# Attention heads on one core: the exponentials turned by fp32 products with the identity instead of transposes

## The chip, the cores and the metric

The kernel runs on one core of a Trainium2 chip. The time is the device time of one execution in microseconds (us). The profile calls the engines PE (TensorE, matrix products; PEld are its weight loads), DVE (VectorE), ACT (ScalarE), POOL (GpSimd) and SP (SyncE). TensorE runs at 2.4 GHz or 1.2 GHz, whichever the chip grants; the profile shows this as a granted clock of 1.00 or 0.50.

## What is computed

Three stages follow each other: an oscillator network with a feed-forward layer, an attention layer with 16 heads of 16 columns over 512 tokens for each of 8 batches, and a mixture of experts. Only the attention is touched:

```
att = einsum('bhqd,bhkd->bhqk', Q, K) / sqrt(Dh) + b[0]
att = att * m + (1.0 - m) * NEG_INF
att = softmax(att, axis=-1)
y = einsum('bhqk,bhkd->bhqd', att, V)
```

TensorE sums over the partition axis. The exponentials come out with the queries q on the partitions, and the product with V needs the keys k there, so each head's 512 x 512 matrix of exponentials has to be turned: 16 tiles of 128 x 128.

## The kernel before

Each engine has its own queue, written out by hand in the function `attention`, and the queues meet only at semaphores. There are 8 x 16 = 128 heads; `all_heads` runs `step(b, h)` over them on each engine. A head is cut into four query tiles (`qt`) and four key tiles (`kc`) of 128.

For head h the work goes round like this:

- PE `scores` (L1021): one product 64 x 128 by 64 x 512 per `qt` into one of two PSUM banks `Lps`. It waits until DVE has emptied that bank two scores ago (`s_neg`).
- DVE `negate_and_max` (L1111): adds the mask term, writes the negated scores `negL` and their minimum `nM` (`s_neg`).
- ACT `exps` (L1081): the exponentials `Pr` in fp32 (`s_exp`).
- PE `transposes` (L1031): for one `kc` it turns the four tiles of `Pr` of the head before into one PSUM bank `Tps[kc]`. The first `kc` of a head waits for all four exponentials of that head (`s_exp`), and each waits for the bank's last reader on DVE (`s_lo`).
- ACT `transposed_high` (L1088) copies `Tps[kc]` to fp16, and DVE `transposed_low` (L1131) writes what the fp16 copy lost.
- PE `values` (L1043, L1046): 32 small products with V, for the head two back; then DVE `invert_sums` (L1119) and `normalize` (L1125), and POOL `split_output` (L979).

The order on PE in one step is score 0, score 1, kc 0 and 1, score 2, kc 2 and 3, score 3, values. The order on ACT is copy of kc 0, copy of kc 1, exponential 0, copy of kc 2, exponential 1, copy of kc 3, exponentials 2 and 3. The order on DVE is minimum 0, minimum 1, low part of kc 0, minimum 2, low part of kc 1, minimum 3, low parts of kc 2 and 3, normalize. Copies and low parts belong to the head before the one whose scores run. When a batch ends, POOL adds up the next batch's mask term `negC` (L947) after the last minimum of the batch, and DVE waits for it before its first minimum of the new batch.

In the first stage the function `transform` (L273) has the program's only other fp32 products: 16 of them, 128 x 128 by 128 x 512, into the tiles the profile calls `up`.

Of the kernel before, what the change touches and what calls it, by code (L numbers as in the profile page):

```python
# [22 lines left out]
P = 128  # L23
# [657 lines left out]
def attention(nc, x1_dram, qk_dram, mask, b0, w_qk, ident, moe_up, WU, YH, YL):  # L681
# [3 lines left out]
    with ExitStack() as ctx:  # L685
        def sb(name, shape, dt=F32):
            return ctx.enter_context(nc.sbuf_tensor(name, shape, dt))
# [9 lines left out]
        with ExitStack() as c1:  # L697
# [30 lines left out]
            @block.sync  # L728
            def _(sp):
                sp.dma_start(wst[:], w_qk).then_inc(in_w, 16)  # L730
                with sp.Fori(0, B // 2) as bb:
                    for j in range(2):
                        b = bb * 2 + j
                        sp.wait_ge(x_lo, b + 1)
                        sp.dma_start(xb[:, j], x1_dram[b]).then_inc(in_x[j], 16)
# [108 lines left out]
        idS = sb("idS", [P, P])  # L844
# [9 lines left out]
        Pr = sb("Pr", [P, 2, DC, D])  # L854
# [5 lines left out]
        Tps = [ctx.enter_context(nc.psum_tensor(f"Tps{i}", [P, 512], F32)) for i in range(4)]  # L860
# [42 lines left out]
        def before(b, h, d):  # L903

            return (b, h - d) if h >= d else (b - 1, h - d + NH)

        def all_heads(eng, step):

            for h in range(NH):
                step(0, h)  # L910
            with eng.Fori(1, B) as b:
                for h in range(NH):
                    step(b, h)
            for h in range(3):
                step(B, h)

        def exists(b, h, d):

            if not isinstance(b, int):
                return True  # L920
            return 0 <= b * NH + h - d < B * NH
# [89 lines left out]
        @block.tensor  # L1011
        def _(pe):
            for s in (s_T, s_pv):
                pe.sem_inc(s, AHEAD)
            pe.wait_ge(in_id, 32)

            def scores(b, h, qt):
                n = (b * NH + h) * DC + qt
                base = 64 * (h % 2)
                pe.wait_ge(s_neg, n - 1 + AHEAD)  # L1020
                pe.matmul(Lps[qt % 2][:, :], QR[base:base + 64, h // 2, qt * P:(qt + 1) * P],  # L1021
                          KR[base:base + 64, h // 2, :], start=True, stop=True).then_inc(s_L, 1)

            def transposes(b, h, kc):
                i = b * NH + h
                if kc == 0:
                    pe.wait_ge(s_exp, i * DC + DC + AHEAD)

                pe.wait_ge(s_lo, DC * i + kc - DC + 1 + AHEAD)
                for qt in range(DC):  # L1030
                    last = pe.transpose(Tps[kc][:, qt * P:(qt + 1) * P], Pr[:, h % 2, qt, kc * P:(kc + 1) * P], idS[:])  # L1031
                last.then_inc(s_T, 1)

            def values(b, h):
                i = b * NH + h
                pe.wait_ge(s_lo, DC * i + DC + AHEAD)
                pe.wait_ge(s_norm, i - 1 + AHEAD)
                for qt in range(DC):


                    out = Ops[h % 2][:, qt]
                    for kc in range(DC):
                        pe.matmul(out[:, 0:VW], PT[:, h % 2, 0, kc, qt * P:(qt + 1) * P], V[:, b, kc, h],  # L1043
                                  start=(kc == 0), stop=False, skip_group_check=True)
                    for kc in range(DC):
                        last = pe.matmul(out[:, DH:VW], PT[:, h % 2, 1, kc, qt * P:(qt + 1) * P], V[:, b, kc, h, DH:VW],  # L1046
                                         start=False, stop=(kc == DC - 1), skip_group_check=True)
                last.then_inc(s_pv, 1)

            def step(b, h):  # L1050
                def score(qt):
                    if exists(b, h, 0):
                        if h % (NH // 2) == 0 and qt == 0:
                            pe.wait_ge(qk_in[h // (NH // 2)], b * QKI + QKI)
                        scores(b, h, qt)

                def transpose(kc):
                    if exists(b, h, 1):
                        transposes(*before(b, h, 1), kc)

                for qt, kcs in ((0, ()), (1, (0, 1)), (2, (2, 3)), (3, ())):
                    score(qt)
                    for kc in kcs:
                        transpose(kc)
                if exists(b, h, 2):
                    values(*before(b, h, 2))

            all_heads(pe, step)
# [372 lines left out]
```

## Time and profile before

| what | value |
|---|---|
| time, median of 3 runs | 3174.29 us (3158.02 to 3213.94) |
| the profiled execution, device time | 3180.47 us |
| its span, first to last instruction | 3178.8 us |
| busy: PE, DVE, POOL, ACT | 85%, 80%, 42%, 39% of the span |
| first and last transpose (L1031) start at | 1801.4 and 2620.0 us |
| granted clock, mean of the span | 0.882 |

Times of single instructions are those of the one profiled execution. A matrix product's duration in the profile runs from its start until its last result is out, so durations of neighbouring products overlap; the spacing of their starts tells how many fit into a stretch. A row "x8" of the timeline merges eight instructions into one piece, from the first start to the last end.

### The profile page before, as it was taken

How to read it: one execution, taken by the hardware profiler on the slowest of the kernel's cores; microseconds unless marked ns; L12 is line 12 of the kernel's file. 1: busy time of each engine (PE TensorE's matmuls, PEld its weight loads, DVE VectorE, ACT ScalarE, POOL GpSimd, SP SyncE). 2: the span in 40 equal slices, each digit the busy share in tenths (PEclk: the TensorE clock that was granted, in tenths of full speed). 3: DMA queues.
4: the chain of work that ended last, by engine and by line, in shares of the span. 5: the costliest groups of instructions: out<-in, count | busy, mean ns of one | idle time of the engine just before them, and what ended most of it. 6: DMA issues, size and time to landing. Idle time of an engine off the chain costs nothing. (4 is left out here: it accounts for less than half of the span.)

```text
span 3178.8 us, 116365 instructions
## 1 busy us (share of the span) xinstructions
PE 2693.4 (85%) x41104; PEld 1859.3 (58%) x41104; DVE 2549.3 (80%) x11914; ACT 1240.1 (39%) x4102; POOL 1350.6 (42%) x3951
## 2 busy tenths in 40 slices
PE   4478888888888888888887788899998995999999
PEld 4356666666666666666665455566665662444444
DVE  7989999999999999999994698877788776544545
ACT  3343333333333333333333587766677660000000
POOL 6845566666565665555552233322333226000000
PEclk6599999999999999999998898855568557999999
DMA  4100000000000000000003411011111101000000
GB/s 177 51 6 10 3 10 10 10 10 7 7 10 10 10 10 4 10 10 10 10 3 127 126 45 43 17 45 32 29 31 45 32 1 67 0 27 26 0 26 13
DMA packets 43922, 88.98 MB, mean 28 GB/s; under 512 B 7168, under 2 KB 23808, under 8 KB 41600
## 3 DMA queue, kind: packets, MB, share of 16 engines
q1 hardware_dynamic: 36336, 63.11, 6.2%
q10 hardware_dynamic: 4752, 10.49, 0.9%
q0 software_dynamic: 2304, 8.39, 0.8%
q8 instruction: 324, 5.31, 0.7%
q14 instruction: 206, 1.69, 0.2%
HBM read 65.18 MB, written 16.78 MB: 26 GB/s over the span
## 5 line engine op out<-in xcount | busy, mean ns | idle before, releaser
L228 PE MATMUL rest<-Tl,CW 128*128 128x56 f16 x16384 | 618.5, 190 | 317.2 <-DVE Tl L494 317.0
L228 PEld LDWEIGHTS rest<-Tl,CW 128*128 128x128 f16 x16384 | 503.1, 97 | 564.2 <-DVE Tl L494 560.2
L347 ACT ACTIVATE Tf<-X 128x32 f32<-128x32 f32 x768 | 176.0, 229 | 781.4 <-DVE X L538 781.4
L1031 PE MATMUL Tps<-idS,Pr 128*128 128x128 f32 x2048 | 421.5, 373 | 52.0 <-ACT Pr L1081 41.9
L1111 DVE CUSTOM_DVE_ANT_0 negL<-Lps,negC 128x512 f32<-128x512 f32 x512 | 341.4, 685 | 140.5 <-PE Lps L1021 133.4
L1031 PEld LDWEIGHTS Tps<-idS,Pr 128*128 128x128 f32 x2048 | 336.1, 193 | 165.3 <-DVE PT L1131 99.8
L1088 ACT ACTIVATE PT<-Tps 128x512 f16<-128x512 f32 x512 | 300.4, 595 | 215.8 <-PE Tps L1031 215.6
L1081 ACT ACTIVATE Pr<-negL,nM 128x512 f32<-128x512 f32 x512 | 361.6, 721 | 21.2 <-DVE nM L1111 17.3
L1131 DVE TENSOR_TENSOR PT<-Tps,PT 128x512 f16<-128x512 f32 x512 | 348.2, 680 | 20.1 <-ACT PT L1088 14.9
L625 POOL TENSOR_TENSOR G<-X,Dr 128x32 f32<-128x32 f32 x768 | 205.8, 268 | 301.9 <-DVE X L499 274.2
L1021 PE MATMUL Lps<-KR,QR 64*128 64x512 f16 x512 | 243.7, 510 | 40.6 <-issue 20.3
L217 PE MATMUL main<-Th,CW 128*128 128x56 f16 x8224 | 264.2, 189 | 10.2 <-DVE CW L450 10.2
L1355 DVE SCALAR_TENSOR_TENSOR moe_acc<-moe_dp,moe_comb,moe_acc 128x512 f32<-128x512 f32 x128 | 96.1, 751 | 193.3 <-PE moe_dp L1255 193.3
L217 PEld LDWEIGHTS main<-Th,CW 128*128 128x128 f16 x8224 | 240.4, 97 | 10.2 <-issue 10.2
L627 POOL TENSOR_SCALAR gm<-X 128x32 f32<-128x32 f32 x768 | 228.0, 297 | 43.0
L524 DVE SCALAR_TENSOR_TENSOR near<-cube,lin 128x32 f32<-128x32 f32 x1024 | 216.1, 211 | 35.2
L979 POOL TENSOR_TENSOR yf<-yn 128x64 f32<-128x64 f32 x128 | 40.9, 320 | 446.7 <-DVE yn L1125 446.7
L1287 ACT ACTIVATE moe_th<-moe_gp 128x512 f32<-128x512 f32 x64 | 38.2, 597 | 486.2 <-PE moe_gp L1241 486.0
L494 DVE TENSOR_TENSOR Tl<-Tf,Th 128x32 f16<-128x32 f32 x1024 | 198.9, 194 | 33.3
L248 PE MATMUL gate<-Xa,WU 128*128 128x128 f16 x3072 | 213.3, 219 | 1.0 <-DVE Xa L546 1.0
L248 PE MATMUL up<-Xa,WU 128*128 128x128 f16 x3072 | 213.1, 219 | 0.0
L490 DVE SCALAR_TENSOR_TENSOR cube<-square,X 128x32 f32<-128x32 f32 x1024 | 210.7, 206 | 0.9 <-issue 0.7
(133 smaller groups left out, 5240.0 us busy)
## 6 DMA issues: line engine op xcount, KB each, us to landing
stage<-w_up SPq DMA_DIRECT2D x8, 1024.0 KB, 4.8
qk<-qkp ACTq DMA_DIRECT2D x32, 256.0 KB, 2.4
QR<-qk SPq DMA_DIRECT2D x128, 64.0 KB, 2.2
KR<-qk SPq DMA_DIRECT2D x128, 64.0 KB, 3.1
wstage<-moe_up POOLq DMA_DIRECT2D x16, 512.0 KB, 5.5
W2m<-w_down SPq DMA_DIRECT2D x1, 4096.0 KB, 13.4
stage<-x_tb SPq DMA_DIRECT2D x16, 256.0 KB, 2.6
x<-stage SPq DMA_DIRECT2D x16, 256.0 KB, 2.1
```

The source lines that it names most:

```text
L217: last = pe.matmul(main[par][:, m], CW[:, wp, k, m * P:(m + 1) * P], Th[:, par, k:k + 1, :].to_broadcast([P, REP, B]), start=(wp == 1 and ...
L228: last = pe.matmul(rest[:, m], CW[:, 0, k, m * P:(m + 1) * P], Tl[:, k:k + 1, :].to_broadcast([P, REP, B]), start=(m == 0 and k == 0), sto ...
L248: ins = pe.matmul(out[:, 0:P], WU[:, hc, which, wp, k, :], Xa[:, xp, k, :], start=(n == 0), stop=(n == 3 * DC - 1))
L490: return own.mark(dve.scalar_tensor_tensor(cube[:], square[:], -3.0, Q, ALU.add, ALU.mult))
L524: own.mark(dve.scalar_tensor_tensor(near[:], cube[:], -a / 3, lin[:], ALU.mult, ALU.add))
L627: own.then_wait(pool.tensor_scalar_mul(gm[:], m, weight))
L1021: pe.matmul(Lps[qt % 2][:, :], QR[base:base + 64, h // 2, qt * P:(qt + 1) * P], KR[base:base + 64, h // 2, :], start=True, stop=True).then ...
L1031: last = pe.transpose(Tps[kc][:, qt * P:(qt + 1) * P], Pr[:, h % 2, qt, kc * P:(kc + 1) * P], idS[:])
L1081: act.activation(Pr[:, h % 2, qt, :], negL[:, qt, :], ACT.Exp, bias=nM[:, h % 4, qt:qt + 1], scale=-1.0).then_inc(s_exp, 1)
L1088: act.activation(PT[:, h % 2, 0, kc, :], Tps[kc][:, :], ACT.Copy).then_inc(s_hi, 1)
L1111: dve.tensor_tensor_reduce(out=negL[:, qt, :], in0=Lps[qt % 2][:, :], in1=negC[:], scale=1.0, scalar=3.0e38, op0=ALU.add, op1=ALU.min, acc ...
L1131: dve.tensor_tensor(PT[:, h % 2, 1, kc, :], Tps[kc][:, :], PT[:, h % 2, 0, kc, :], ALU.subtract).then_inc(s_lo, 1)
```

## The change

One call in `transposes` is replaced. The operands and the place of the result stay the same: the tile of `Pr` is the stationary operand, the identity `idS` the moving one, and the result lies in `Tps[kc]`. All waits and the order of all queues stay.

```
             for qt in range(DC):
-                last = pe.transpose(Tps[kc][:, qt * P:(qt + 1) * P], Pr[:, h % 2, qt, kc * P:(kc + 1) * P], idS[:])
+                last = pe.matmul(Tps[kc][:, qt * P:(qt + 1) * P], Pr[:, h % 2, qt, kc * P:(kc + 1) * P], idS[:], start=True, stop=True)
             last.then_inc(s_T, 1)
```

## Rows read from the trace of the kernel before

**Rows 1.** The page: busy time of PE, and granted clock in 40 slices.
```profile
PE 2693.4 (85%) x41104; PEld 1859.3 (58%) x41104; DVE 2549.3 (80%) x11914; ACT 1240.1 (39%) x4102; POOL 1350.6 (42%) x3951
PEclk6599999999999999999998898855568557999999
```

**Rows 2.** Line 1031: duration in ns (least/median/most), first and last start.
```profile
L1031 PE MATMUL Tps<-idS,Pr x2048: 272/418/478, 1801.4 to 2620.0; 128*128 128x128 f32 x187
```

**Rows 3.** Windows: length, busy PE, PEld, DVE, ACT, POOL; clock; DMA share, GB/s.
```profile
1886.00:1892.00 6.00, 5.24 (x63) 3.46 (x61) 6.00 (x18) 5.10 (x11) 2.01 (x5) 1.00 0.88 251
2076.00:2345.00 269.00, 262.39 (x1988) 172.84 (x1987) 206.45 (x537) 184.70 (x307) 75.93 (x152) 0.50 0.13 35
2346.00:2458.00 112.00, 93.10 (x980) 64.22 (x979) 97.84 (x262) 85.45 (x149) 38.09 (x73) 0.86 0.15 41
```

**Rows 4.** Timeline, one head at clock 0.50: start us, length us, engine, line.
```profile
2202.61 1.97 PE L1031 MATMUL Tps<-idS,Pr 128*128 128x128 f32 x8
2204.52 0.61 PE L1021 MATMUL Lps<-KR,QR 64*128 64x512 f16 x1
2205.05 1.97 PE L1031 MATMUL Tps<-idS,Pr 128*128 128x128 f32 x8
2206.95 0.60 PE L1021 MATMUL Lps<-KR,QR 64*128 64x512 f16 x1
...
2209.43 0.47 PE L1031 MATMUL Tps<-idS,Pr 128*128 128x128 f32 x1
...
2206.20 0.60 ACT L1088 ACTIVATE PT<-Tps 128x512 f16<-128x512 f32 x1 [0.37 <-PE Tps L1031]
2206.70 0.71 ACT L1081 ACTIVATE Pr<-negL,nM 128x512 f32<-128x512 f32 x1
2207.31 0.59 ACT L1088 ACTIVATE PT<-Tps 128x512 f16<-128x512 f32 x1
2207.78 1.50 ACT L1081 ACTIVATE Pr<-negL,nM 128x512 f32<-128x512 f32 x2
...
2207.83 0.69 DVE L1111 CUSTOM_DVE_ANT_0 negL<-Lps,negC 128x512 f32<-128x512 f32 x1 [1.13 <-PE Lps L1021]
```

**Rows 5.** Timeline, one head at clock 1.00.
```profile
1900.90 1.09 PE L1031 MATMUL Tps<-idS,Pr 128*128 128x128 f32 x8 [0.59 <-ACT Pr L1081]
1901.99 0.39 PE L1021 MATMUL Lps<-KR,QR 64*128 64x512 f16 x1
1902.31 1.09 PE L1031 MATMUL Tps<-idS,Pr 128*128 128x128 f32 x8
1903.33 0.39 PE L1021 MATMUL Lps<-KR,QR 64*128 64x512 f16 x1
...
1906.29 1.09 PE L1031 MATMUL Tps<-idS,Pr 128*128 128x128 f32 x8 [0.89 <-DVE PT L1131]
...
1901.67 1.08 ACT L1088 ACTIVATE PT<-Tps 128x512 f16<-128x512 f32 x2 [0.90 <-PE Tps L1031]
```

**Rows 6.** Timeline around the end of a batch, clock 0.50.
```profile
2291.28 1.97 PE L1031 MATMUL Tps<-idS,Pr 128*128 128x128 f32 x8
...
2300.47 1.03 PE L1021 MATMUL Lps<-KR,QR 64*128 64x512 f16 x2 [3.27 <-issue]
2301.43 1.97 PE L1031 MATMUL Tps<-idS,Pr 128*128 128x128 f32 x8
```

**Rows 7.** The other fp32 products: timeline at full and half clock, and line 273.
```profile
161.09 1.10 PE L273 MATMUL up<-W2m,hadS 128*128 128x512 f32 x2
...
188.89 2.06 PE L273 MATMUL up<-W2m,hadS 128*128 128x512 f32 x2
...
L273 PEld LDWEIGHTS up<-W2m,hadS x32: 187/191/338, 147.4 to 189.0; 128*128 128x128 f32 x32
L273 PE MATMUL up<-W2m,hadS x32: 592/676/1202, 147.5 to 189.9; 128*128 128x512 f32 x32
```

**Rows 8.** Windows of the first stage, just before and while these products run.
```profile
120.00:147.00 27.00, 11.13 (x212) 9.98 (x210) 25.90 (x84) 7.44 (x30) 22.00 (x35) 0.50 0.11 40
147.00:182.00 35.00, 23.80 (x328) 12.59 (x325) 28.23 (x124) 20.73 (x71) 15.69 (x43) 0.95 0.09 32
```

## The prediction

> **What bounds the kernel now.** I read the page first. PE is busy 85% of the span, but the slices show that its clock is near full everywhere except around the heads, where it falls to 0.5 to 0.6 [rows 1]. The edit touches only line 1031, whose 2048 transposes run from 1801.4 to 2620.0 us [rows 2]. So only these 818.6 us can change.
>
> Next I read the windows. The heads run in two ways. At clock 1.00 DVE is busy 6.00 of 6 us [rows 3], and a head takes 1906.29 - 1900.90 = 5.39 us [rows 5]: DVE's queue is the bound. At clock 0.50 PE is busy 262 of 269 us and DVE only 206 [rows 3], and a head takes 2209.43 - 2202.61 = 6.82 us [rows 4]. About half of the stage runs like this. The window 2346 to 2458, clock 0.86, lies between.
>
> What sets 6.82 us is a loop, read from the timeline [rows 4]. The last exponential of a head releases kc 0 and 1 (2202.61); after them comes score 2 (2204.52), kc 2 and 3 (2205.05), score 3 (2206.95), then minimum 3 on DVE (2207.83), which had waited 1.13 us for it, then exponential 3 on ACT, and with its end the next head's kc 0 (2209.43). All 16 transposes lie on this loop. At full clock the same loop is shorter than 5.39 us and DVE hides it.
>
> **What the change costs.** It removes 2048 transposes and adds 2048 fp32 products. Nothing else moves: no DMA, no wait, no order.
>
> *One transpose.* Eight of them take 1.09 us at full clock and 1.97 us at half clock [rows 4, 5]; the difference of 0.88 us is 0.11 us each. Taking 0.16 us of run-out off the 0.272 us of one record gives the same: a transpose holds PE for 0.109 us at full clock and 0.213 us at half.
>
> *One product.* The trace has no fp32 product of 128 columns. The nearest is line 273: 128 x 128 weights, 512 columns. Each product is two records of weights and two of products [rows 7]. The undisturbed record lasts 0.592 us; less 0.166 us of run-out (0.39 us of a 512-column score less the 0.213 us that it streams is 0.17 [rows 5]) leaves 0.426 us for half of it, so 0.853 us for 512 columns and 0.213 us for 128. That is the lower bound. The first record is longer by 0.084 us (0.676), because its weights were not there yet. The whole pair takes 1.10 us, a quarter of which is 0.275 us. As an upper bound I take weights that hide behind nothing: two loads of 0.188 us, 0.376 us. Between these ends I take two times 0.109 = 0.218 us, since the second load of line 273 lay wholly behind the running product, and since the transposes, whose weights are also fp32, come one every 0.109 us. The product is then twice as dear as the transpose at the same clock, and as dear as a transpose at half clock.
>
> *Which clock.* A head with products streams, in columns at 2.4 GHz: 16 x 0.213 + 4 x 0.213 (scores) + about 0.8 us of values, some 5.1 us in 6.5 us. In the window 147 to 182 us the products of line 273 came into a stretch that had been at 0.50, and the clock there was 0.95 with PE busy 24 of 35 us; before them it was 0.50 [rows 8]. Twice the streaming in the heads speaks for the full clock throughout. The Trainium skill ("TensorE: Matmul & The Clock Gate", Part 4) says that the full clock does not engage for transposes, since they do not count as work the same way; the trace agrees in part, as 269 us at 0.50 with PE nearly always busy show [rows 3], though other heads with the same transposes had 1.00. By that page too the products would bring the full clock.
>
> *The loop with products at full clock*, step by step:
>
> - kc 0 and 1: transposes took 1.02 us up to the score behind them (1902.31 to 1903.33 [rows 5]); 8 x 0.109 = 0.87 more, and 0.05 for a longer first load: 1.94 us.
> - score 2 to kc 2: 1901.99 to 1902.31 [rows 5]: 0.32 us.
> - kc 2 and 3: 1.94 us.
> - score 3 to minimum 3: 2206.95 to 2207.83 is 0.88 us at half clock; the score is 0.39 us instead of 0.60 [rows 4, 5]: 0.67 us.
> - minimum 3 to exponential 3: the pair ends at 2209.28, its second half of 0.72 us begins at 2208.56: 0.73 us [rows 4].
> - exponential 3 to the next kc 0: 2208.56 to 2209.43, a little less at full clock: 0.85 us.
>
> This sums to 6.45 us. A second path through ACT is nearly as long. From the start of kc 2, its four products and the run-out take 1.09 us, and ACT follows 0.11 us behind (in rows 5: 1900.90 + 0.06 + 4 x 0.109 + 0.16 is 1901.56, the copy starts at 1901.67). From there the copy of kc 2, exponential 1, copy of kc 3, exponentials 2 and 3 follow each other at 0.50, 0.61, 0.47 and 0.61 us [rows 4], so exponential 3 starts 3.39 us after kc 2, where the first path says 1.94 + 0.67 + 0.73 = 3.34. I take 6.50 us for a head.
>
> DVE needs 5.39 us of this and is hidden; POOL is far from its bound. What was hidden behind DVE at full clock, the loop over PE, becomes the bound there; where the clock was at half, the score products and the gaps get shorter and the turning itself stays the same.
>
> *The batches.* At a batch's end PE waits 3.27 us for its next scores [rows 6], and 10.15 us pass from head to head instead of 6.82. Six such places (a seventh is not seen) cost about 20 us in all; they depend on POOL and DVE, and I leave them: 0.16 us per head.
>
> *Sum.* 127 x (6.50 + 0.16) + 3.6 us for the last head is 849 us, against 818.6: 31 us more. On the profiled execution's own 3180.5 us this gives 3211 us. That execution lies 0.2% above the median of 3174.29 us; the runs spread from 3158 to 3214 us, which fits stages with more or fewer heads at half clock (each costs 1.43 us more). With products the stage has no such choice, so I leave 3211 us as it is: 1.2% above the median. 2%, which is about what a measurement of this kernel can tell from no change, is reached at 3238 us, with 6.71 us per head or 0.231 us per product. That is close.
>
> **The rivals.**
>
> - *DVE stays the bound, faster.* PE had 0.6 to 0.9 us of idle time before each kc 0 at full clock [rows 5], and the products would keep the clock at 1.00 for all heads. If a product cost under 0.148 us (6.50 less 16 x 0.07 is 5.38), every head would take 5.39 us: 127 x 5.55 + 3.6 = 708 us, so 3070 us. Against it stand the 0.426 us of half a product [rows 7]. 5%.
> - *The first load of each product is not hidden.* Line 273 shows 0.084 us of it each time [rows 7], there after products too short to hide it. If this holds in a row of products, 16 x 0.084 = 1.34 us per head and 171 us are added: 3382 us. 9%.
> - *A product costs four transposes.* 0.436 us each at full clock, 3.49 us more per head: 3654 us. Only the two records of 0.426 us speak against it; nothing shows 128 columns. 3%. The Trainium skill ("TensorE: Matmul & The Clock Gate", Terms) puts the transpose mode at 4 times as fast for fp32; the trace's columns say 2.
> - *The clock stays at half.* Products at 0.427 us make 6.82 + 16 x 0.213 = 10.24 us per head and 3890 us. Rows 8 speak against it. 3%.
> - *The edit does nothing*, the identity product being run as the transpose was: about 3174 us. 2%.
>
> **The numbers.** My forecast holds with 78%, at 3185 to 3260 us: 0.01 us on a product is 20 us, 0.1 us on the rest of the loop 13 us. Of this I put 48% within 2% and 30% above. The range from 3170 to 3300 us leaves out the first four rivals, 20%, and takes in a load that is hidden in part. Faster by over 2% is the first rival, 5%; within 2% is 48 + 2 = 50%; slower is 30 + 9 + 3 + 3 = 45%.
>
> **What would show it.** Line 1031 has 4096 records of products, one each 0.109 us; eight products take about 1.9 us. The clock is 1.00 from the first batch to the last, and no head takes 5.39 us any more. Heads take 6.5 us all through, DVE waits for score 3 for about 1 us, and the stage lasts about 849 us. I am wrong if the records in a burst lie 0.15 us or more apart, if the clock falls within the stage, or if something else than this loop sets the period.

## The result and the profile after

The changed kernel takes 3222.6 us (median of 4 runs, 3220.4 to 3224.1), the kernel before 3173.8 us in the same comparison (3158.0 to 3213.9). The ratio is 1.0185 (95% interval 1.0126 to 1.0244): slower by 1.3 to 2.4%, so slower, but whether by more than 2% is open. The kernel before spreads over 56 us, the changed one over 4.

That spread matters for every ratio below. In the later comparisons the kernel before took 3192.2 us (7 runs, 3145.4 to 3220.7), 3198.8 us (7 runs, 3190.6 to 3228.0) and 3195.7 us (13 runs, 3157.6 to 3229.7). Ratios leave out runs of a kernel that lie more than 1.5% above its fastest, so the same 3077 us is 0.9728 of it in one comparison and 0.9584 in another. The changed kernel was not run again beside these; against 3195.7 us it would be 0.8% slower.

The page of the changed kernel: busy time, clock in 40 slices, and line 1031 for products and weight loads. They answer to [rows 1].

```profile
span 3221.7 us, 120461 instructions
PE 2745.6 (85%) x43152; PEld 2004.5 (62%) x43152; DVE 2555.6 (79%) x11914; ACT 1242.9 (39%) x4102; POOL 1351.8 (42%) x3951
PEclk6599999999999999999998899999999997999999
L1031 PE MATMUL Tps<-idS,Pr 128*128 128x128 f32 x4096 | 537.0, 285 | 51.7 <-ACT Pr L1081 51.5
L1031 PEld LDWEIGHTS Tps<-idS,Pr 128*128 128x128 f32 x4096 | 488.2, 195 | 123.4 <-DVE PT L1131 78.2
```

TensorE has 2048 records more. In the kernel before, six slices of the heads had stood at 5 or 6 tenths; here the slices inside the stage of the heads are all at 9. The same line by its durations, to be read against [rows 2]:

```profile
L1031 PE MATMUL Tps<-idS,Pr x4096: 274/275/582, 1797.3 to 2662.6; 128*128 128x128 f32 x196
```

The stage lasts 865.3 us instead of 818.6, so 46.7 us more; the rest of the span is 3.8 us shorter. That accounts for the spans, 3221.7 and 3178.8 us.

One head of the changed kernel in the timeline (start us, length us), first PE, then ACT, then DVE. It answers to [rows 4, 5].

```profile
2202.32 2.05 PE L1031 MATMUL Tps<-idS,Pr 128*128 128x128 f32 x16 [0.44 <-ACT Pr L1081]
2204.30 0.39 PE L1021 MATMUL Lps<-KR,QR 64*128 64x512 f16 x1
2204.61 2.05 PE L1031 MATMUL Tps<-idS,Pr 128*128 128x128 f32 x16
2206.60 0.39 PE L1021 MATMUL Lps<-KR,QR 64*128 64x512 f16 x1
...
2207.81 0.60 PE L1021 MATMUL Lps<-KR,QR 64*128 64x512 f16 x2
2208.85 0.37 PE L1031 MATMUL Tps<-idS,Pr 128*128 128x128 f32 x1 [0.43 <-ACT Pr L1081]
...
2205.81 0.60 ACT L1088 ACTIVATE PT<-Tps 128x512 f16<-128x512 f32 x1 [0.20 <-PE Tps L1031]
2206.30 0.71 ACT L1081 ACTIVATE Pr<-negL,nM 128x512 f32<-128x512 f32 x1
2206.91 0.59 ACT L1088 ACTIVATE PT<-Tps 128x512 f16<-128x512 f32 x1
2207.39 1.33 ACT L1081 ACTIVATE Pr<-negL,nM 128x512 f32<-128x512 f32 x2
...
2207.26 0.69 DVE L1111 CUSTOM_DVE_ANT_0 negL<-Lps,negC 128x512 f32<-128x512 f32 x1 [0.64 <-ACT Pr L1081]
```

From 2202.32 to 2208.85 is 6.53 us for a head. Eight products, now sixteen records, run 2.05 us, and the clock is full: the score lasts 0.39 us. Minimum 3 on DVE (2207.26) had to wait, and its exponential is the second of the pair that ends at 2208.72. The row names an exponential as releaser, but the one that it has to wait for is of the head before and had long been done; score 3 ended at 2206.99, and minimum 3 follows it by 0.27 us; in [rows 4] it follows by 0.28 us (2207.55 and 2207.83).

The end of a batch, PE in the timeline and one window (length, PE, PEld, DVE, ACT, POOL, clock, DMA), answers to [rows 6]:

```profile
2217.67 2.05 PE L1031 MATMUL Tps<-idS,Pr 128*128 128x128 f32 x16
2219.66 0.39 PE L1021 MATMUL Lps<-KR,QR 64*128 64x512 f16 x1
...
2224.25 1.03 PE L1021 MATMUL Lps<-KR,QR 64*128 64x512 f16 x2 [3.32 <-issue]
2225.21 3.78 PE L1031 MATMUL Tps<-idS,Pr 128*128 128x128 f32 x16
...
2222.00:2230.00 8.00, 5.75 (x25) 4.49 (x26) 2.83 (x8) 1.56 (x3) 2.48 (x6) 0.57 0.61 182
```

PE idles 3.32 us, where it had idled 3.27 in [rows 6]. There the clock was at half already; here it was full and falls after the pause (0.57 in the window), and the next eight products take 3.78 us instead of 2.05.

### The profile page after: what moved, and what is told of

It reads as the page before. It is cut to its first block and busy times, and to the rows that moved or that the text cites. A ratio compares the mean times of both kernels' runs of the same rounds, so it can differ in the third digit from the quotient of the medians.

```text
span 3221.7 us, 120461 instructions
## 1 busy us (share of the span) xinstructions
PE 2745.6 (85%) x43152; PEld 2004.5 (62%) x43152; DVE 2555.6 (79%) x11914; ACT 1242.9 (39%) x4102; POOL 1351.8 (42%) x3951
## 5 line engine op out<-in xcount | busy, mean ns | idle before, releaser
L1031 PE MATMUL Tps<-idS,Pr 128*128 128x128 f32 x4096 | 537.0, 285 | 51.7 <-ACT Pr L1081 51.5
L1031 PEld LDWEIGHTS Tps<-idS,Pr 128*128 128x128 f32 x4096 | 488.2, 195 | 123.4 <-DVE PT L1131 78.2
L1081 ACT ACTIVATE Pr<-negL,nM 128x512 f32<-128x512 f32 x512 | 352.4, 715 | 17.0 <-DVE nM L1111 17.0
L1021 PE MATMUL Lps<-KR,QR 64*128 64x512 f16 x512 | 180.4, 393 | 37.8 <-issue 20.2
```

The lines of the kernel that those rows point to most:

```text
L1031: last = pe.matmul(Tps[kc][:, qt * P:(qt + 1) * P], Pr[:, h % 2, qt, kc * P:(kc + 1) * P], idS[:], start=True, stop=True)
L1081: act.activation(Pr[:, h % 2, qt, :], negL[:, qt, :], ACT.Exp, bias=nM[:, h % 4, qt:qt + 1], scale=-1.0).then_inc(s_exp, 1)
```

## The experiments

### Two transposes in place of one product

```
                 for qt in range(DC):
-                    last = pe.transpose(...)
+                    for _ in range(2):
+                        last = pe.transpose(...)
```

> Every tile is turned by two transposes into the same place instead of one fp32 product, so TensorE has the same number of records and the same streaming as after the change, but no product. Theory A (only the streaming counts, for the time and for the clock): 4096 records one each 0.109 us, clock near 1.00 through the heads, 6.5 us per head, about 3222 us like the changed kernel. Theory B (transposes don't count as work for the clock): the clock stays at 0.50, each record 0.213 us, 6.82 + 16 x 0.213 = 10.2 us per head, near 3700 to 3900 us.

3203.6 us (3201.2 to 3208.7), 1.0128 of the kernel before in its own comparison (1.0012 to 1.0244). The page's clock slices and one head in the timeline:

```profile
PEclk6599999999999999999998899999999997999999
...
2146.80 1.96 PE L1032 MATMUL Tps<-idS,Pr 128*128 128x128 f32 x16 [0.45 <-ACT Pr L1082]
2148.69 0.39 PE L1021 MATMUL Lps<-KR,QR 64*128 64x512 f16 x1
...
2153.18 1.09 PE L1032 MATMUL Tps<-idS,Pr 128*128 128x128 f32 x8 [0.45 <-ACT Pr L1082]
```

The slices are the same as with products. With 4096 transposes in place of 2048 the clock is as full as with the products, so theory B falls. The Trainium skill ("TensorE: Matmul & The Clock Gate", Part 4), which I weighed in the prediction, says that the full clock does not engage for transposes; these slices do not bear that out. A head takes 6.38 us (2146.80 to 2153.18). The burst up to the score is 1.89 us, with products 1.98 us (2202.32 to 2204.30): 0.09 us per burst, two bursts per head, accounts for the 0.15 us between 6.38 and 6.53. No other difference between a product and two transposes shows.

### Only part of the tiles by products

```
                 for qt in range(DC):
-                    last = pe.transpose(...)
+                    if kc == 3:        # second kernel: kc >= 2
+                        last = pe.matmul(..., start=True, stop=True)
+                    else:
+                        last = pe.transpose(...)
```

> Only key tile 3 (4 of the 16 tiles of a head) is turned by products, the other 12 by transposes as before. Theory A (the loop over PE and DVE's queue compete, the longer one is the bound, and the added streaming lifts the clock): the loop at full clock is 6.53 - 12 x 0.109 = 5.22 us, under DVE's 5.39, so 5.39 us per head; if the clock holds at 1.00 everywhere about 3222 - 127 x 1.14 = 3077 us. If the clock still falls in part of the heads, 3077 plus about 2 us for each such head. Theory C (each product adds its share, whatever the clock): a quarter of the way from 3174 to 3222, 3186 us.

> Key tiles 2 and 3 by products, 0 and 1 by transposes. Theory A: the loop over PE is 6.53 - 8 x 0.109 = 5.66 us, now longer than DVE's 5.39, clock 1.00: 5.66 us per head and 3222 - 127 x 0.87 = 3112 us. If PE's total work or DVE alone were the bound and no loop, 5.39 us per head, 3077 us. Theory C (share by share): 3198 us.

With key tile 3 alone: 3076.6 us (3075.3 to 3079.6), 0.9728 of the kernel before (0.9618 to 0.9838). That is the 3077 of theory A, and theory C, which says slower, falls: a quarter of the change makes the kernel faster. A window of it away from a batch's end shows why (length, PE, PEld, DVE, ACT, POOL, clock, DMA, as in [rows 3]):

```profile
1886.00:1960.00 74.00, 64.35 (x779) 48.08 (x780) 71.76 (x193) 61.50 (x110) 28.34 (x55) 1.00 0.13 36
```

The clock is 1.00 and DVE is busy 72 of 74 us, as it had been only in parts of the kernel before [rows 3].

With key tiles 2 and 3: 3131.6 us (3130.8 to 3133.2), 0.9899 (0.9788 to 1.0011), 20 us above my 3112. A head takes 5.79 us and not 5.66. The timeline shows a path I had left out (PE, then DVE):

```profile
2205.70 1.09 PE L1034 MATMUL Tps<-idS,Pr 128*128 128x128 f32 x8 [0.43 <-ACT Pr L1084]
2206.95 0.39 PE L1021 MATMUL Lps<-KR,QR 64*128 64x512 f16 x1 [0.16 <-DVE nM L1114]
...
2206.20 0.68 DVE L1114 CUSTOM_DVE_ANT_0 negL<-Lps,negC 128x512 f32<-128x512 f32 x1
2206.81 0.08 DVE L1114 DVE_READ_ACCUMULATOR2_ANT nM<- 128x1 f32 x1
```

Score 2 waits for minimum 0 (done at 2206.89), since they share a bank, and minimum 0 stands in DVE's queue behind minimum 3, two low parts and normalize. With all tiles by products score 2 comes late anyhow, and this path does not matter. The head's 0.13 us above my sum are 17 of the 20 us.

### More work where TensorE is idle

```
             def scores(b, h, qt):
...
-                pe.matmul(Lps[qt % 2][:, :], ...).then_inc(s_L, 1)
+                for _ in range(3 if qt == 1 else 1):
+                    last = pe.matmul(Lps[qt % 2][:, :], ...)
+                last.then_inc(s_L, 1)
```

> The kernel before with its transposes; score 1 of each head is computed three times into the same bank, which adds 1024 columns of work where TensorE is idle at full clock. Theory A (the heads at 6.82 us are slow only because the clock is at half, and the clock follows the streaming): clock 1.00 through the heads, 5.39 us per head although PE does more, about 3077 us, below both kernels. Rival (the clock does not follow the streaming, or the heads at 6.82 us have another cause): the extra work lies on the loop at half clock, about 7.5 us per such head, above 3200 us.

3105.2 us (3089.0 to 3106.4), 0.9799 (0.9679 to 0.992). Two useless products of 512 columns per head make the kernel faster than before. They do it only in part: the window that answers to the second of [rows 3]:

```profile
2076.00:2345.00 269.00, 242.17 (x2473) 157.54 (x2472) 238.25 (x637) 208.16 (x366) 92.39 (x180) 0.89 0.13 36
```

The clock there is 0.89 where it was 0.50, not 1.00. Which kind of work lifts the clock how much is not told apart by this run.

### Which path closes the loop

```
-                for qt, kcs in ((0, ()), (1, (0, 1)), (2, (2, 3)), (3, ())):
+                for qt, kcs in ((0, ()), (1, (0, 1)), (2, (2,)), (3, (3,))):
```

This is made on the changed kernel: score 3 is moved ahead of key tile 3.

> The changed kernel (all tiles by products) with score 3 moved ahead of key tile 3 on TensorE; nothing else moves. Theory A2 (two paths of equal length close the loop: score 3 to minimum 3 on DVE, and the copies of key tiles 2 and 3 on ACT ahead of the last exponentials): the first path gets 0.9 us shorter, but the copy of key tile 3 comes 0.32 us later, so 6.53 + 0.32 = 6.85 us per head, near 3260 us. Rival (only the path over score 3 and minimum 3 bounds): 5.65 us per head, near 3110 us.

3261.7 us in one run, which was not repeated. PE and ACT in the timeline:

```profile
2206.26 2.05 PE L1031 MATMUL Tps<-idS,Pr 128*128 128x128 f32 x16 [0.66 <-ACT Pr L1081]
...
2213.11 2.05 PE L1031 MATMUL Tps<-idS,Pr 128*128 128x128 f32 x16 [0.66 <-ACT Pr L1081]
...
2211.16 0.60 ACT L1088 ACTIVATE PT<-Tps 128x512 f16<-128x512 f32 x1 [0.20 <-PE Tps L1031]
2211.66 1.32 ACT L1081 ACTIVATE Pr<-negL,nM 128x512 f32<-128x512 f32 x2
```

A head takes 6.85 us (2206.26 to 2213.11). The copy of key tile 3 (2211.16) now waits for PE, and the last two exponentials stand behind it. Score 3 came earlier and that gained nothing, so the path over ACT bounds as well as the one over DVE, as the prediction's 3.39 and 3.34 us said.

### Key tile 3 turned twice by transposes

```
-                    last = pe.transpose(...)
+                    for _ in range(2 if kc == 3 else 1):
+                        last = pe.transpose(...)
```

> The kernel before, where only the four tiles of key tile 3 are turned twice by transposes into the same place; no product at all. Theory A (the gain of the version with products in key tile 3 is the clock, and that follows the streaming alone): 5.39 us per head, clock 1.00 but for the batch ends, near 3077 us, below the kernel before. Rival (products are needed to hold the clock): a third to a half of the heads at half clock, 3150 us or more.

3076.7 us (3073.4 to 3078.2), 0.9584 of the kernel before in that comparison (0.9512 to 0.9655). With products in the same place it was 3076.6 us. The clock slices:

```profile
PEclk6599999999999999999999889999999998999999
```

The slices inside the stage of the heads are all at 9 again. No product is needed; the added work alone keeps the clock up.

### The end of a batch

Two kernels on top of the one with key tile 3 by products: the mask term summed by DVE (L947's work), and TensorE's heads written out without a loop.

```
-                if h == 0 and real:       # POOL
-                    mask_sum(b)
...
                 if h == 0 and exists(b, h, 0):       # DVE
+                    dve.wait_ge(negc_t, 3 * b + 3)
+                    dve.wait_ge(s_neg, 64 * b + AHEAD)
+                    dve.sem_inc(halt, 1)
+                    dve.tensor_tensor(negC[:], mt[:, 0], mt[:, 1], ALU.subtract).then_inc(negc_ok, 1)
```

> Key tile 3 by products, the rest by transposes, and the mask term of a new batch is summed up by DVE itself instead of POOL. Theory P (the 3.3 us at a batch's end are PE's own, the jump back to the start of its loop and the loading of its instructions): no gain, 3077 us within 5. Rival M (the wait is for POOL's sum, as my prediction had it): the 3.3 us and the short fall of the clock after them go, 7 times, 3045 us.

3081.1 us (3077.5 to 3084.4): no gain. PE's waits (us in total, times, longest us) still have the pause:

```profile
PE Lps L1011 <- issue: 20.4, 6, 3.5
```

So rival M falls.

```
-            all_heads(pe, step)
+            for b in range(B):
+                for h in range(NH):
+                    step(b, h)
+            for h in range(3):
+                step(B, h)
```

> Key tile 3 by products, the rest by transposes, and TensorE's program for the heads is written out for all eight batches, without a loop; the other engines keep theirs. Theory P (the jump back costs the 3.3 us): no idle time of 3.3 us and no fall of the clock at a batch's end, 5.2 us less at each of seven places, near 3045 us. Rival M (POOL's sum): 3077 us, unchanged.

3072.3 us (3069.9 to 3072.6): 4 us gained and not 32, so theory P fails too in this form, in which TensorE's jump back alone costs the 3.3 us. What DVE waited for in it, and then in the kernel in which the same edit is made in `all_heads`, for all four engines (us in total, times, longest us):

```profile
DVE negL L1118 <- issue: 18.4, 7, 3.3
DVE negL L1118 <- PE Lps L1021: 14.1, 11, 1.9
...
DVE negL L1112 <- POOL negC L945: 2.5, 7, 0.7
DVE negL L1112 <- PE Lps L1019: 1.7, 2, 1.4
```

With TensorE's loop gone DVE idles without a releaser; six of the seven waits are of 2.8 to 3.3 us and stand at the batches' ends, the seventh is short. At these ends DVE's own loop jumps back: its seven turns, for the second to the eighth batch, have six jumps between them.

> Key tile 3 by products, the rest by transposes, and the head programs of all four engines are written out for the eight batches, without a loop. The version with TensorE alone written out gained 5 us, not 33, and its trace shows DVE idle for up to 3.3 us without a releaser at seven places. Theory P2 (every engine's own jump back costs about 3 us, and they overlap, so taking away one uncovers the next): now the wait at a batch's end and the fall of the clock go, 5.35 us per head, stage 683 us, near 3045 us. Rival M2 (at a batch's end POOL's sum or the loads of q and k hold everything up as well): 3065 us or more.

3033.7 us (3031.0 to 3033.9), 0.9464 of the kernel before (0.9385 to 0.9542). The six long waits are gone, and what is left is 2.5 us for POOL's sum. The loads of q and k are as they were, so rival M2 falls too. A window of the heads, and two heads in PE's timeline:

```profile
1815.00:2490.00 675.00, 595.57 (x7233) 438.64 (x7230) 651.42 (x1768) 562.23 (x1000) 263.25 (x508) 0.99 0.15 44
...
2200.59 1.09 PE L1032 MATMUL Tps<-idS,Pr 128*128 128x128 f32 x8 [0.47 <-ACT Pr L1082]
...
2205.84 1.09 PE L1032 MATMUL Tps<-idS,Pr 128*128 128x128 f32 x8 [0.47 <-ACT Pr L1082]
```

The clock is 0.99 from the first batch to the last. A head takes 5.25 us (2200.59 to 2205.84), less than the 5.39 with a loop, which explains why the time is 11 us under what I expected.

A head outside a loop is shorter in the kernel before as well. Its first batch is written out ahead of the loop, and two heads of it at full clock start 5.24 us apart:

```profile
1818.81 1.09 PE L1031 MATMUL Tps<-idS,Pr 128*128 128x128 f32 x8 [0.56 <-ACT Pr L1081]
...
1824.05 1.09 PE L1031 MATMUL Tps<-idS,Pr 128*128 128x128 f32 x8 [0.70 <-ACT Pr L1081]
```

With TensorE alone written out most heads take 5.32 us. Why a head in a loop is longer was not tried.

The same on the changed kernel, all tiles by products:

> The changed kernel (all tiles by products) with the head programs of all four engines written out, without a loop. Theory P2: all heads take 6.53 us, the excess of some 5 us at each batch's end is gone, stage 127 x 6.53 + 3.6 = 833 us, near 3190 us, that is at most 0.5% above the kernel before and its loops. Rival M2: 3210 us or more.

3188.4 us (3182.8 to 3189.3), 1.0005 of the kernel before (0.9976 to 1.0034), and 34 us less than the changed kernel with its loops. A window of the heads, and two heads in PE's timeline:

```profile
1805.00:2630.00 825.00, 776.02 (x8672) 631.61 (x8670) 682.34 (x1776) 599.22 (x1017) 257.11 (x508) 1.00 0.11 31
...
2202.18 2.05 PE L1029 MATMUL Tps<-idS,Pr 128*128 128x128 f32 x16 [0.36 <-ACT Pr L1079]
...
2208.64 2.05 PE L1029 MATMUL Tps<-idS,Pr 128*128 128x128 f32 x16 [0.36 <-ACT Pr L1079]
```

The clock is 1.00 and a head takes 6.46 us instead of 6.53. The kernel before, with its transposes, was not run without loops, so what the change costs there is not known.

## Why the prediction was right, and where it was off

- **What bounds.** Right. At half clock the loop over TensorE, at full clock DVE. The kernel with key tile 3 lands at 5.39 us and the changed one at 6.53, as the two say, and the move of score 3 lands at 6.85 us. With key tiles 2 and 3 a head takes 5.79 us where the two say 5.66: the path over minimum 0 was missing from the prediction.
- **The product.** I took 0.218 us. Eight run in 2.05 us against 1.96 us for sixteen transposes, and up to the score a burst takes 1.98 us where the sum had 1.94. The first load of each product is hidden: the rival with 0.084 us per product would make a head 7.8 us. The rival of four transposes is out as well. The Trainium skill ("TensorE: Matmul & The Clock Gate", Terms) gives 4 times for the transpose mode in fp32; the runs say 2.
- **The clock.** Right for the heads: full through all batches. At the six batch ends it fell, though, which was one of the prediction's own signs of being wrong; what that cost is counted below. The gain and the loss are both in the sum. Heads that took 6.82 us got 0.29 us shorter, heads that took 5.39 us 1.14 us longer.
- **The loop.** 6.53 us against 6.50 predicted: 4 us over the stage.
- **The ends of batches.** This is the term that was mis-sized. I left the 20 us as they were and put them on POOL and DVE. In the changed kernel thirteen of the 127 spacings from head to head are long. One is the very first head, 8.82 us, which started at half clock: 2 us more than the others (the window from 1797 to 1802 us is at 0.50). The other twelve are two at each of the six ends, 109.1 us together; less 12 x 6.53 that is 31 us. PE's idle time stayed (3.27 us in [rows 6], 3.22 to 3.59 here), but as the clock now falls behind it, the burst of products that follows takes 3.12 to 3.78 us instead of 2.05. In the kernel before, three of the six ends lay in stretches at half clock, where there was nothing to fall, and the 3.33 us that I took for all six come from one of these. At another end its clock fell and stayed down:

```profile
2068.54 1.09 PE L1031 MATMUL Tps<-idS,Pr 128*128 128x128 f32 x8 [0.78 <-ACT Pr L1081]
...
2075.59 0.86 PE L1021 MATMUL Lps<-KR,QR 64*128 64x512 f16 x2 [3.41 <-issue]
2076.38 1.97 PE L1031 MATMUL Tps<-idS,Pr 128*128 128x128 f32 x8
```

  With this pause begin the 269 us at 0.50 of [rows 3]; in the changed kernel the clock is full again one or two bursts after each end.
- **Their cause.** It was not POOL's sum, since the sum on DVE gained nothing, but the ends of the engines' loops. Writing the loops out shortened the stage by 39 us with products (865.3 to 826.7) and by 44 us with key tile 3 alone (715.6 to 672.0). Not all of that is the ends: the some 111 heads that had stood in a loop are shorter by 0.07 us, which makes 8 us of the first, and by 0.15 us, which makes 17 us of the second. The ends are the rest, some 31 and 27 us.
- **The sum.** 849 us predicted for the stage, 865.3 measured: 11 us from the batches' ends, 2 us from the first head and 4 us from the others, less 1 us for those of the first batch, which take 6.46. The rest of the span gave 4 us back, which no step of the prediction foresaw; that is luck. Hence 3222.6 us where I had 3211.
- **A slip in a rival.** The clock that stays at half was priced at 3890 us. By its own terms, 10.24 us per head where the sum has 6.50, it comes to 3211 + 127 x 3.74 = 3686 us. It did not come true, and no other number rests on it.
- **The first rival**, DVE stays the bound, did not come for all tiles: a product costs 0.22 us, not under 0.148. DVE does stay the bound, and heads take 5.39 us, when only a quarter of the tiles is made dearer.

## What to carry to other kernels

When TensorE is busy nearly all the time at half clock, look for what a little more work on it would do: here making a quarter of the tiles twice as dear took 3 to 4% off the time (0.9728 and 0.9584 in two comparisons), and doubling the work on all tiles gave it back, because then TensorE's loop was longer than DVE's queue. Cost a change on TensorE at the clock that the changed kernel will have, and find every path that closes the loop; with key tiles 2 and 3 by products, 5.39 us (DVE's queue), 5.66 us (the loop, by the sum) and 5.79 us (the path over minimum 0) lie within 0.4 us. Where several engines loop in step, writing out one of them can only uncover the pause of the next: TensorE alone gained 4 us, all four together 43. How many of the four it takes was not tried.

## What the runs showed of the hardware

- An fp32 product of 128 x 128 by 128 columns comes one every 0.22 us at full clock, as two weight loads and two products; an fp32 transpose one every 0.109 us, as one of each. A burst of sixteen transposes is 0.09 us shorter than one of eight products (1.89 and 1.98 us up to the score).
- Transposes hold the full clock as products do: 4096 of them in the place of 4096 product records gave the same clock slices.
- A TensorE that is nearly always busy can stay at half clock: 262 of 269 us at 0.50 in [rows 3]. More work of the same kind lifted it: with four of the sixteen tiles turned twice, the slices inside the stage are all at 9.
- At the end of a loop of 16 heads TensorE stops for 3.2 to 3.8 us, six times in every run with its loop, and DVE for 2.8 to 3.3 us where TensorE no longer does; written out, both are gone. ACT's and POOL's share was not told apart. What an engine does in that time no run here tells.
- A head in a loop takes 0.15 us more than one written out (5.39 and 5.24 us), 0.07 us of it from TensorE's loop.
